# A transformer layer on one Trainium2 core: feed-forward and attention-output products as whole float32 products, relu squared on GpSimd

## What is computed

```python
x = x + attention(layernorm(x), Wq, Wk, Wv, Wo)      # 16 heads, window 128, token 0 sees and is seen by all
h = _bitlinear(x', w_fc) + gate * (x' @ v.T @ fast_b.T @ u.T)      # x' = layernorm(x); hidden width 1024, rank 16
r = jnp.maximum(h, 0.0)
x = x + _bitlinear(r * r, w_proj)
# _bitlinear: x @ (ternary(w) * scale).T, scale = mean |w| over each row of w, ternary in {-1, 0, 1}
```

## Time and profile before

| | |
|---|---|
| median of 3 runs | 1153.78 us (1153.77 to 1153.89) |
| span of the profiled execution | 1152.4 us |
| TensorE (PE) busy | 1126.9 us, 98% |
| VectorE (DVE) busy | 979.5 us, 85% |
| ScalarE (ACT) busy | 843.4 us, 73% |
| GpSimd (POOL) busy | 706.8 us, 61% |
| mean granted TensorE clock | 0.994 of full speed |

### The profile page before, as it was taken

The page is one execution under the profiler, slowest core; times in us unless marked ns, Lnnn a source line. Parts: engine busy times, 40 slices in busy tenths (PEclk is TensorE's granted clock), DMA queues, the critical chain, the costliest instruction groups (busy, mean ns, idle before and its releaser), DMA issues.

```text
span 1152.4 us, 26576 instructions
## 1 busy us (share of the span) xinstructions
PE 1126.9 (98%) x9115; PEld 785.0 (68%) x9115; DVE 979.5 (85%) x3169; ACT 843.4 (73%) x1513; POOL 706.8 (61%) x935
## 2 busy tenths in 40 slices
PE   9999997999999999999999999999999999999998
PEld 8888884455555555555555455558888988898887
DVE  7889857899889998899889999867888888888885
ACT  7989983788888888888788888875465546554654
POOL 3665565677778777887778877773344334433443
PEclk9999998999999999999999999999999999999999
DMA  6999897555555555545565554240232113211201
GB/s 199 295 296 281 257 266 168 114 131 118 137 133 122 132 125 136 132 115 137 126 138 130 114 138 108 68 139 29 74 102 64 56 55 102 64 55 56 74 20 37
DMA packets 158166, 145.24 MB, mean 126 GB/s; under 512 B 21564, under 2 KB 157776, under 8 KB 158032
## 3 DMA queue, kind: packets, MB, share of 16 engines
q1 hardware_dynamic: 158032, 143.54, 48.8%
HBM read 91.74 MB, written 50.95 MB: 124 GB/s over the span
## 4 chain that ended last, share of the span: by engine, by line
PE 73%; DVE 7%; issue 2%; ACT 1%; POOL 1%; DVEq 0%; POOLq 0%; ACTq 0%
PE e_psum L1549 15%; PE e_psum L1503 15%; PE e_psum L1527 14%; PE e_psum L1844 6%; PE e_psum L1846 5%; PE e_psum L1267 3%; PE e_psum L1825 3%; PE e_psum L1824 3%; DVE n_stats L142 2%; DVE f_x L1958 2%; PE e_psum L1829 1%; PE e_psum L255 1%; PE e_psum L254 1%; PE e_psum L253 1%; PE e_psum L1793 1%
## 5 line engine op out<-in xcount | busy, mean ns | idle before, releaser
L1665 DVE CUSTOM_DVE_ANT_0 a_masked<-e_psum,band 128x387 f32<-128x387 f32 (+1 forms) x1024 | 493.3, 534 | 58.8 <-PE e_psum L1503 55.8
L1622 ACT ACTIVATE a_weights<-e_psum 128x1024 f32<-128x1024 f32 (+1 forms) x512 | 398.0, 806 | 87.2 <-PE e_psum L1527 82.2
L1401 POOL TENSOR_SCALAR_AFFINE_SELECT a_weights<-a_weights 128x1024 f32<-128x1024 f32 x256 | 276.2, 1091 | 59.9 <-ACT a_weights L1622 58.7
L1503 PE MATMUL e_psum<-e_k,e_q 96*128 96x387 bf16 (+1 forms) x1024 | 281.4, 327 | 3.0 <-PEq L281 1.4
L1888 POOL TENSOR_TENSOR f_square<-f_relu 128x512 f32<-128x512 f32 x128 | 146.1, 1142 | 209.6 <-ACT f_relu L1877 198.6
L1527 PE MATMUL e_psum<-e_q,e_k 128*128 128x384 bf16 (+2 forms) x1408 | 255.6, 279 | 1.5 <-ACT a_weights L1622 1.1
L1549 PE MATMUL e_psum<-a_weights,a_v 128*17 128x384 f32 (+2 forms) x2816 | 195.8, 392 | 1.0 <-POOL a_weights L1401 1.0
L1527 PEld LDWEIGHTS e_psum<-e_q,e_k 128*128 128x128 bf16 x1408 | 129.0, 98 | 95.6 <-issue 39.5
L1503 PEld LDWEIGHTS e_psum<-e_k,e_q 96*128 96x128 bf16 x1024 | 100.4, 98 | 99.2 <-DVE a_max L1665 44.8
L1844 PE MATMUL e_psum<-w_w_t,f_square_hi 128*128 128x256 f32 x512 | 129.4, 287 | 5.6 <-DVE f_square_lo L1934 5.6
L1846 PE MATMUL e_psum<-w_w_t,f_square_lo 128*128 128x256 f32 x512 | 126.8, 282 | 0.0
(11 more groups left out here) (219 smaller groups left out, 2059.0 us busy)
## 6 DMA issues: line engine op xcount, KB each, us to landing
k_parts<-p_k_parts SPq DMA_DIRECT2D x48, 258.0 KB, 4.6
e_k<-k_parts SPq DMA_DIRECT2D x64, 193.5 KB, 3.6
e_k<-k_parts SPq DMA_DIRECT2D x192, 64.5 KB, 3.3
q_parts<-p_q_parts SPq DMA_DIRECT2D x48, 256.0 KB, 5.1
e_q<-q_parts SPq DMA_DIRECT2D x64, 192.0 KB, 3.7
e_q<-q_parts SPq DMA_DIRECT2D x192, 64.0 KB, 3.3
v_ones<-p_va SPq DMA_DIRECT2D x16, 544.0 KB, 5.9
p_x<-in_x SPq DMA_DIRECT2D x16, 512.0 KB, 6.3
```

Source lines behind the costliest of these rows:

```text
L1401: pool.affine_select(out=blocks, in_=blocks, compare_op=ALU.is_ge, fill=0.0, base=0, pattern=[[0, NQ // 2 * HEAD_COLS // P // CUT_STEP], [ ...
L1503: pe.matmul(sh.tile_bank(ux, j)[:, lo:hi], qw[ux.q][0:SLOT_ROWS, h, t * P:t * P + P], kt[ux.hq][0:SLOT_ROWS, h, start + lo:start + hi], st ...
L1622: act.activation(pe_w[:, us.upar, lo:hi], score[c % 2][:], ACT.Exp).then_inc(s_exp, 1)
L1665: dve.tensor_tensor_reduce(out=masked[:, ux.upar, h, t:t + hi - lo], in0=bank[:, lo:hi], in1=band[:, lo:hi], scale=1.0, scalar=NEG, op0=AL ...
```

## The change

Every split is dropped. The weights are made whole while they are prepared: the row scale and the rank-16 part go into `w1_t` (a float32 product with a diagonal of the scales, plus one of the two low-rank factors), the column scale goes into `w2_t`. The rows, the squares and the attention rows are kept as one float32 tile each, and each product is one `matmul` of float32 operands in place of the two, three or five before. ScalarE takes only the relu, GpSimd squares it, VectorE no longer subtracts anything in the feed-forward and adds the output straight to the residual. In the feed stage:

```diff
-                ins = three_pass(pe, self.attention_bank(q, c)[:, t * D:t * D + D],
-                                 [sh.ot_hi[:, k, part] for k in range(KT)], [sh.ot_lo[:, k, part] for k in range(KT)],
-                                 [w.wo_hi[:, k, :] for k in range(KT)], [w.wo_lo[:, k, :] for k in range(KT)])
+                for k in range(KT):
+                    ins = pe.matmul(self.attention_bank(q, c)[:, t * D:t * D + D], sh.ot[:, k, part], w.wo_t[:, k, :],
+                                    start=(k == 0), stop=(k == KT - 1))
...
-    def pe_ternary(self, pe, q, j):
+    def pe_hidden(self, pe, q, j):
+        if j == 0:
+            pe.wait_ge(self.s_xtc, q.g * KT + KT)
         wait(pe, self.s_r, q.g * MH + j - 1)
         for k in range(KT):
...
+            ins = pe.matmul(self.h_bank[j % 2][:], self.w.w1_t[:, k, j * P:j * P + P], self.sh.xt[:, q.par, k, :],
+                            start=(k == 0), stop=(k == KT - 1))
+        ins.then_inc(self.s_h, 1)
...
-                pe.matmul(y, sh.r2_hi[:, j % 4, part], self.w.w2_t[:, j, :], start=(j == 0 and t == 0), stop=False,
-                          skip_group_check=True)
-                ins = pe.matmul(y, sh.r2_lo[:, j % 4, part], self.w.w2_t[:, j, :], start=False, stop=(j == MH - 1),
-                                skip_group_check=True)
+                ins = pe.matmul(y, sh.r2[:, j % 4, part], self.w.w2_t[:, j, :], start=(j == 0 and t == 0),
+                                stop=(j == MH - 1), skip_group_check=True)
...
-        act.activation(sh.r[:, j % 4, :], self.h_bank[j % 2][:], ACT.Relu, scale=self.w.mag[:, j:j + 1]
-                       ).then_inc(self.s_r, 1)
-        act.wait_ge(self.s_r, q.g * MH + j + 1)
-        act.activation(sh.r2_hi[:, j % 4, :], sh.r[:, j % 4, :], ACT.Square).then_inc(self.s_r2hi, 1)
+        act.activation(sh.r[:, j % 4, :], self.h_bank[j % 2][:], ACT.Relu).then_inc(self.s_r, 1)
...
-            dve.tensor_tensor(self.scaled[:, c], self.y_bank[c][:], self.w.mag_row[:], ALU.mult).then_inc(self.s_yc, 1)
...
+            dve.tensor_tensor(rows, self.y_bank[c][:], rows, ALU.add).then_inc(self.s_fin, 1)
```

In the preparation of the weights:

```diff
     def pe_w1(self, pe, n):
...
+        pe.matmul(bank[:], self.low_b[:, k * P:k * P + P], self.u_t[:, c * GT:(c + 1) * GT], start=True, stop=False,
+                  skip_group_check=True)
         for m in range(TB):
-            ins = pe.transpose(self.ring[(2 + n) % 4][:, m * P:m * P + P],
-                               self.w1_in[:, c * TB + m, k * P:k * P + P], self.ident[:])
+            ins = pe.matmul(bank[:, m * P:m * P + P], self.w1_in[:, c * TB + m, k * P:k * P + P],
+                            self.diag1[:, c * TB + m, :], start=False, stop=(m == TB - 1), skip_group_check=True)
...
             for m in range(KT):
-                ins = pe.transpose(self.ring[n][:, i * D + m * P:i * D + m * P + P],
-                                   self.w2_in[:, m, (2 * n + i) * P:(2 * n + i + 1) * P], self.ident[:])
...
+                ins = pe.matmul(self.ring[n][:, i * D + m * P:i * D + m * P + P],
+                                self.w2_in[:, m, (2 * n + i) * P:(2 * n + i + 1) * P], self.mag_diag[:, m, :],
                                 start=True, stop=True)
...
-            idle_products(total_bank, 10)
```

More of the change, by code:

```diff
@@ L682, in _ @@
                            ).then_inc(s_rexp, 1)
+            weights.act_w1(act, 0)
+            weights.act_w1(act, 1)
         @block.vector
@@ L1167, in __init__ @@
             over("fill1", [P, fill])
-            self.xt_hi, self.xt_lo = over("xt_hi", [P, 2, KT, GT], F32R), over("xt_lo", [P, 2, KT, GT], F32R)
+            self.xt = over("xt", [P, 2, KT, GT])
+            over("hole3", [P, 2 * KT * GT])
             over("fill2", [P, fill])
-            self.r, self.r2 = over("relu", [P, 4, GT]), over("square", [P, 4, GT])
+            self.r = over("relu", [P, 4, GT])
+            over("hole4", [P, 4 * GT])
             over("fill3", [P, fill])
@@ L1560, in body @@
                         weights.pe_w1(pe, 2 + j // 2)
-                    if ux and ux.n == 0 and j in (5, 7):
-                        weights.pe_u(pe, j // 2 - 2)
-                    if ux and ux.n == 0 and j in (9, 11, 13, 15):
-                        weights.pe_w2(pe, j // 2 - 4)
-                    if ux and ux.n == 1 and j == 3:
-                        weights.pe_mag(pe)
+                    if ux and ux.n == 0 and j in (5, 7, 9, 11):
+                        weights.pe_w2(pe, j // 2 - 2)
                     for kind, n in AFTER_TILE[j]:
@@ L1597, in _ @@
                 weights.act_w1(act, n)
-            for n in range(2):
-                weights.act_u(act, n)
             for n in range(4):
@@ L1633, in body @@
                 if uo and uo.n == UNITS - 2:
-                    feed.act_norm_high(act, Group(0))
+                    feed.act_norm_copies(act, Group(0))
                 if um and um.n == 0:
-                    weights.act_mag(act)
                     act.wait_ge(weights.s_pc, weights.COPIES)
@@ L1776, in pe_turn_o @@
         for k in range(KT):
-            wait(pe, self.s_lo, (q.g - 2) * KT + k + 1)
-            if z and k == 0:
-                pe.wait_ge(self.s_zlo, z.g + 1)
+            wait(pe, self.s_xtc, (q.g - 2) * KT + k + 1)
             for t in range(TB):
@@ L1949, in dve_last @@
             rows = self.x1_rows(q, c)
-            dve.tensor_tensor(self.scaled[:, c], self.y_bank[c][:], self.w.mag_row[:], ALU.mult).then_inc(self.s_yc, 1)
-            dve.wait_ge(self.s_yc, q.g * 2 + c + 1)
-            dve.tensor_tensor(rows, self.scaled[:, c], rows, ALU.add).then_inc(self.s_fin, 1)
-    def dve_final(self, dve, q):
-        for c in range(2):
-            dve.wait_ge(self.s_yc, q.g * 2 + c + 1)
-            rows = self.x1_rows(q, c)
-            dve.tensor_tensor(rows, self.scaled[:, c], rows, ALU.add).then_inc(self.s_fin, 1)
+            dve.tensor_tensor(rows, self.y_bank[c][:], rows, ALU.add).then_inc(self.s_fin, 1)
 def stage_feed(block, feed):
@@ L2007, in body @@
             if qf:
-                feed.pe_low_rank(pe, qf)
-                feed.pe_ternary(pe, qf, 0)
-                feed.pe_ternary(pe, qf, 1)
+                feed.pe_hidden(pe, qf, 0)
+                feed.pe_hidden(pe, qf, 1)
                 if qf.g == 0:
                     sh.pe_sums_turned(pe, Unit(UNITS - 1))
-                feed.pe_low(pe, qf, 0)
-                feed.pe_low(pe, qf, 1)
             if qa:
-                feed.pe_turn_o(pe, qa, qf)
+                feed.pe_turn_o(pe, qa)
             if qf:
                 for j in range(2, MH):
-                    feed.pe_ternary(pe, qf, j)
-                    feed.pe_low(pe, qf, j)
+                    feed.pe_hidden(pe, qf, j)
                     if j >= 3:
@@ L2063, in body @@
             qa, qx, qf, qb = at(0), at(LX), at(LF), at(LB)
[L2064 to L2070 removed]
+            if qb:
                 feed.dve_final(dve, qb)
```

256 lines of the change are left out of this document (75 added, 181 removed).

## The result

The changed kernel took 1316.55 us (median of 3; 1314.42 to 1316.63) against 1153.78: a ratio of 1.14, 95% interval [1.138, 1.1421]. The forecast was 1308.0 with 1301 to 1329, so it held; the point was 8.5 us low. The span of the profiled execution is 1312.7 us at a mean clock of 0.991.

The account below looks back on a forecast made before the run. TensorE's stream was taken to bound the feed stage. The terms 1.2 + 2.5 + 0.4 (end of attend) + 151.6 - 1.5 = 154.2 raise the span from 1152.4 to 1306.6; 1.4 from span to median gives 1308.0 us, range 1301 to 1329.

Parts of the forecast that it names:

- Two records for a product, and their distance: TensorE: a float32 product is two records, 0.430 us each for 512 columns and 0.216 for 256.
- A: Rival: a whole float32 product passes TensorE's array as one record, step 17.3 us, about 1061 us; chance 0.03.
- B: Rival: large float32 records are slowed by reading, 0.465 and 0.238 us each, 35.7 us a step, 1353 us; chance 0.06.
- C: Rival: weight loads of 0.19 us stand in front of each feed-stage record, +334, 1642 us; chance 0.01.
- No wait in the step: Feed stage: TensorE should not wait at all in a step of 32.8 us.
- D: Rival: TensorE keeps a wait for the squares, 0.8 us a step, +12, 1320 us; chance 0.05.
- The feed stage: Fourteen steps of 32.8 us, then 28.4 and 27.6, make 514.9 us against 363.3: +151.6 us.
- The tail: Behind the last product: the last add ends 0.75 us after it instead of 2.3, -1.5 us.
- The weights before attend: Two weight blocks stand where ten idle products stood, so L581 starts 1.2 us later (0 to +2).
- the first units: Start of attend, score tiles alternating with weight blocks on TensorE: +2.5 us; +0.8 at full clock throughout.
- I take one at either level: First units of attend: one `pe_w1` block at full and one at half clock, 5.2 against 2.0 us, +3.2.
- At half clock throughout +7: First units of attend: upper bound of their loss if the clock is half throughout, +7 us instead of +2.5.

Follow-up runs that it names:

- run with one record: The changed kernel with its six operand tiles in float32r instead of float32, so each product is one record; 1008.39 us, ratio 0.875 to the kernel before.
- run with the attention alone: The kernel before with only the attention output as one float32 product per pair of blocks and VectorE's low part there dropped; 1161.37 us, ratio 1.007.
- run with 128 rows: The changed kernel with the low-rank product's factors filled up with zeros from 16 to 128 rows; 1306.87 us, ratio 1.1331 to the kernel before.
- The last run: The changed kernel in float32r, attention product ahead of the norm's transposes, statistics ahead of the residual add, low-rank product with 128 rows; 971.6 us, ratio 0.8425.
- the second series: The changed kernel measured again, the same program, beside the two kernels that alter only its weight preparation; 1314.28 us.

## Why the prediction was right, and where it was off

- **Two records for a product, and their distance: right.** 1024 and 512 records; 0.430 and 0.216 us, as the line through the earlier trace rows gave. Rivals A (one record, 1061 us) and B (0.465 and 0.238) fall on these rows. The run with one record is not A: its records are float32r ones at 0.12 us for 256 columns, where A had 0.216. Of what was cited against A, the Trainium skill (FP8 and Floating Point Precision, TensorE Precision Notes) states the four passes of true float32; this trace has two records and 3.7 times the time of a float32r product, and that the reduced form is one record is the trace's word.
- **Weight loads beside the products: right.** L1774's loads are 190 ns each, 1024 of them, and the distance stays 0.216; C falls.
- **No wait in the step: right.** TensorE's idle time before L1758 and L1774 is 0.0; D falls. The run with the attention alone shows the same in small: the work taken off VectorE returned nothing.
- **The feed stage: right.** 794.23 to 1309.16 (the end of the last record's slot) is 514.9 us, as forecast. The steps of 32.75, then 28.4 and 27.6, are the count. That it agrees to a tenth is in part luck: the first step takes 33.19, with four transposes of attend's sums (L1224) that the count left out, and the other thirteen 0.03 less each than counted. Taken apart, the output products measured +89 us by themselves, where the count gives (13.82 - 64 x 0.119) x 16 less the waits of 12, 87.
- **The tail: right.** 0.71 us behind the last product; 0.75 was said.
- **The weights before attend (+1.2) and the first units (+2.5): the work was counted rightly, its clock and the price of one product were wrong.** L580 began 2.67 us later than L581 before (175.29), took 8.47 us in place of 7.53, and the feed stage began at 794.23, 10.3 us later where the sum had 4.1: 3.6 arise up to the end of L580, where 1.2 stood, and 6.7 behind it, where 2.5 + 0.4 stood. The difference is the whole error in the span (1312.7 against 1306.6). The step that was off is "I take one at either level": I took one of two blocks at half clock, for the fall that the earlier trace rows showed already, and held that the new products, keeping TensorE busy, would leave the clock alone. Both blocks of `pe_w1` there and the first of `pe_w2` (1.70 us) ran at half, and before attend, where no fall was priced at all, so did the last products of the second block and the start of L580. The other step is the 1.75 us for a block: it priced L1040 at 0.430 a record, which is the price with 128 rows. With its 16 rows, at full clock, the first block took 2.14 us (170.34 to 172.48), and 1.85 in the run with 128 rows.
- **The same terms without the 16 rows.** The run with 128 rows has L581 at 173.94 (+1.3) and feed at 786.55 (+2.6 where 1.2 + 0.8 + 0.4 = 2.4 was worked out for full clock throughout). The last run, also with 128 rows, has the mixed case: its two blocks take 3.47 us at half clock and 1.75 at full, 5.2 together, as worked out. So the terms were sound for the clock and the rows that they assumed. Of the 7.7 us between 794.23 and 786.55, 2.3 arise before attend and 5.4 in its first unit. From the first score tile there to the first one behind the last weight block it is 14.7 us in each of the three profiles with 16 rows (the changed kernel twice, the run with one record), and 9.3 and 11.0 in the two with 128. The 1.7 us between those two are a fall that comes with 128 rows as well, so 6.0 of the 7.7 us go with the 16-row shape in every profile here and 1.7 need not.
- **A bound that doesn't follow.** "At half clock throughout +7" is too low by its own terms: 6.8 - 2.0 for `pe_w1`, 4 x (2.35 - 0.96) for `pe_w2` (2.35 is a block with its two tiles as it ran at half clock, 195.51 to 197.86), less 1.8, is 8.6. The range held without it.
- **The rest of the 8.5 us** is the step from span to median: 1.4 us was taken from before, while the profiled execution was the lowest of the three here (1314.42; 1.7 above its span). In the second series the median was 1314.28.

Why the clock falls with few rows stays open. The profiles show this: around the weight blocks before attend it fell to 0.50 in all three with 16 rows and in neither with 128; at the start of attend it was at 0.50 for some 10 us in all three with 16 rows, and with 128 rows for some 3 us in one and not at all in the other. The Trainium skill (TensorE: Matmul & The Clock Gate, Part 1) ties the clock to how busy the engine has been; a stretch at 0.50 with TensorE busy 8.00 of 8.00 us doesn't fit that, if busy is what the profile calls so.

## What to carry to other kernels

Count records, not products, and read the distance between starts from the chain: a float32 product costs as much as 3.7 float32r ones here, so a split into two or three reduced products is cheaper than one whole product, and dropping work on engines that TensorE doesn't wait for pays nothing. Give a product with few rows zero rows up to 128 when it stands in a stream (16 rows here, worth 6 to 8 us). Before moving an operation on VectorE, look at what GpSimd does at its new place, and when a wait of TensorE has grown, look at the granted clock behind it.

## What the runs showed of the hardware

- Float32 products of 16 rows went with a fall of the granted clock to 0.50 while TensorE was busy without a gap (8.00 of 8.00 us in 188 to 196); with 128 rows the mean clock there was 1.00 in one run and 0.85 in another.
- At full clock a float32 record of 16 rows and 512 columns stands 0.517 us from the next, one of 128 rows 0.429.
- Where TensorE waited for a low part for 0.31 us in each step (the kernel before), the clock stayed at 1.00 through the feed stage. Where that wait was 1.96 or 2.44 us, the clock fell to 0.50 for some 3 us in 7 and in 10 of 14 steps, which cost some 1.55 us each time.
- A VectorE operation with both inputs in SBUF takes about 1.06 us in the mean beside GpSimd's squares, where it takes 0.65 alone, and the squares go from 1.04 to 1.38.
